# Causal attention with a routed feed-forward layer on one core: the masked key tiles of a head group move from its end to its start

## The reference, cut to what matters

```python
x = x + attention(layernorm(x), w_qkv, w_out)
x = x + ffn(layernorm(x), ...)

# attention: rotary position on q and k, then
scores = einsum('bhqd,bhkd->bhqk', q, k) * dh ** -0.5
scores = where(causal, scores, finfo.min)
out = einsum('bhqk,bhkd->bhqd', softmax(scores), v) @ w_out
# ffn: base_W product + a shared rank-16 pair + the best 2 of 6 routed rank-16 pairs, weighted by a softmax gate
```

## Time and profile before

| | |
|---|---|
| median of 3 runs | 338.3 us (334.99 to 338.99) |
| the profiled execution | 338.65 us |
| its span, first to last instruction | 336.9 us |
| exponentials (L465) | 272, one every 0.9 us where nothing holds them up |
| idle time of ACT before them | 40.1 us |

### The profile page before, as it was taken

How to read it: one execution, slowest core, us unless ns; L and a number is a source line. 1 busy time by engine, 2 the same in 40 slices (tenths; PEclk the granted TensorE clock), 3 DMA queues, 4 the chain that set the end, 5 groups by cost and what they waited for, 6 DMA issues and landing times.

```text
span 336.9 us, 6044 instructions
## 1 busy us (share of the span) xinstructions
PE 305.3 (91%) x2327; PEld 95.2 (28%) x2329; DVE 139.9 (42%) x406; ACT 270.1 (80%) x285; POOL 56.8 (17%) x134
## 2 busy tenths in 40 slices
PE   7968779897998999789999999999999999999985
PEld 2422222223333422223322312223122212421453
DVE  6863771597337557852651102002400400210463
ACT  9907375895978798698999999999999999899000
POOL 0524343030311300300303012003003003002000
PEclk9985997797999999999999999999999999999999
DMA  7260333022600010330000100000000000100001
GB/s 200 82 177 5 93 90 103 1 53 63 167 2 2 0 35 2 94 93 2 0 2 2 32 2 3 0 2 0 2 0 3 1 2 0 33 0 2 2 0 31
DMA packets 13586, 11.66 MB, mean 35 GB/s; under 512 B 1825, under 2 KB 12306, under 8 KB 13554
## 3 DMA queue, kind: packets, MB, share of 16 engines
q1 hardware_dynamic: 13410, 10.84, 11.7%
q0 software_dynamic: 144, 0.39, 0.4%
HBM read 3.88 MB, written 1.05 MB: 15 GB/s over the span
## 4 chain that ended last, share of the span: by engine, by line
PE 44%; DVE 22%; ACT 18%; issue 13%; DMA 2%; POOL 0%; DVEq 0%; ACTq 0%
PE po L745 18%; ACT pbuf L465 18%; PE ps L719 11%; DVE rest L526 3%; PE pm L782 3%; PE pm L768 2%; PE pm L771 2%; DVE rest L540 2%; PE ps L850 1%; DVE rot L532 1%; DVE xn L505 1%; PE pm L786 1%; PE pm L774 1%; DVE rot L519 1%; DVE parts L538 1%
## 5 line engine op out<-in xcount | busy, mean ns | idle before, releaser
L465 ACT ACTIVATE pbuf<-ps 128x1024 f32<-128x1024 f32 x272 | 253.9, 1122 | 40.1 <-PE ps L719 39.8
L745 PE MATMUL po<-pbuf,va 128*9 128x512 f32 (+3 forms) x1280 | 146.2, 541 | 1.7 <-DVE oT L513 1.3
L719 PE MATMUL ps<-qst,kst 64*128 64x512 bf16 (+3 forms) x640 | 99.2, 361 | 7.2 <-ACT pbuf L465 2.3
L444 POOL TENSOR_SCALAR_AFFINE_SELECT pbuf<-pbuf 128x256 f32<-128x256 f32 (+1 forms) x112 | 49.9, 461 | 242.1 <-ACT pbuf L465 241.5
L719 PEld LDWEIGHTS ps<-qst,kst 64*128 64x128 bf16 x640 | 25.3, 94 | 128.7 <-ACT pbuf L465 107.1
L513 DVE COPY oT<-po 128x512 f32<-128x512 f32 x16 | 11.0, 690 | 63.8 <-PE po L745 63.6
L745 PEld LDWEIGHTS po<-pbuf,va 128*9 128x9 f32 x1280 | 21.3, 89 | 49.9 <-issue 42.1
L587 DVE COPY xnT<-pm 128x512 f32<-128x512 f32 x12 | 8.3, 692 | 28.0 <-PE pm L768 28.0
L607 DVE RECIPROCAL rec<-pm 128x16 f32<-128x16 f32 x16 | 4.1, 258 | 34.7 <-PE pm L782 34.7
L850 PE MATMUL ps<-kst 128*128 128x512 bf16 x55 | 13.0, 379 | 0.2 <-issue 0.2
L771 PE MATMUL pm<-xnT,wqkv 128*128 128x512 f32 x16 | 10.1, 714 | 2.7 <-DVEq L636 2.7
(11 more groups left out here) (90 smaller groups left out, 181.6 us busy)
## 6 DMA issues: line engine op xcount, KB each, us to landing
kst<-parts SPq DMA_DIRECT2D x23, 128.0 KB, 2.5
qst<-parts SPq DMA_DIRECT2D x22, 128.0 KB, 2.4
xs<-x_dram SPq DMA_DIRECT2D x4, 256.0 KB, 3.4
cosT<-rope_c_dram SPq DMA_DIRECT2D x4, 256.0 KB, 4.2
sinT<-rope_s_dram SPq DMA_DIRECT2D x4, 256.0 KB, 4.8
out_dram<-xs SPq DMA_DIRECT2D x4, 256.0 KB, 2.3
wqkv<-w_qkv_dram SPq DMA_DIRECT2D x1, 320.0 KB, 4.1
qst<-parts POOLq DMA_DIRECT2D x2, 128.0 KB, 3.0
```

The costliest lines, as they stand in the source:

```text
L444: ins = nc.gpsimd.affine_select(out=edge, in_=edge, compare_op=ALU.is_ge, fill=0.0, base=0, pattern=[[0, edge.shape[1]], [1, P]], channel_ ...
L465: nc.scalar.activation(pbuf[:, u % NPB, :], ps[:, u % NS, :, :].rearrange("p b q -> p (b q)"), ACT.Exp, scale=SCALE).then_inc(exp_ready, 1)
L719: ins = nc.tensor.matmul(ps[:, u % NS, e, at * 2 * P + place:at * 2 * P + place + n], side(kst, e)[:, g * 2 + pair, key:key + P], side(qst ...
L745: ins = nc.tensor.matmul(po[32 * j:32 * j + DH + 1, q0:q0 + n], va[:, blk["kt"] + dk, head, :], pbuf[:, buf % NPB, at:at + n], start=blk[" ...
```

## The change

One line of the plan changes: within a group the order was old key tiles 0 to 4c-1, diagonal `full`, `ends`, `mid`. It is now diagonal `full`, `ends`, `mid`, then the old key tiles from 0 up. In chunk 0 there are no old tiles, and nothing changes. The number of units and blocks, `LAG`, the places of the jobs and of the evacuations, and every instruction's shape stay.

```diff
-            work = [("full", kt) for kt in range(4 * c + 1)] + [("ends", 4 * c + 1), ("mid", 4 * c + 2)]
+            work = [("full", 4 * c), ("ends", 4 * c + 1), ("mid", 4 * c + 2)] + [("full", kt) for kt in range(4 * c)]
```

## The result

The changed kernel took 343.24 us (median of 4 runs, 340.08 to 344.39), the kernel before beside it 338.36 us. The ratio is 1.0172, with a 95% interval of 1.0116 to 1.0228: slower, by 1.2 to 2.3%. The ratios leave out executions in a slower state and the medians do not, so a ratio is not the quotient of two medians (here 1.0144). The profiled execution took 343.01 us, its span is 341.3 us against 336.9.

What follows compares the result with a forecast made beforehand. ACT's exponentials (246 us) and 40 us of PE being late with scores were taken to bound the kernel; 1.0 + 0.6 + 1.9 - 0.3 + 0.2 = +3.4 us gave 341.7 us, eight-in-ten range 337.0 to 345.0.

Steps and rivals of the forecast that it cites:

- N10: Chunk 1: the wait before this job loses the block that filled it; PE idle 0.5 us, scores of 51 0.5 later.
- O0: Chunk 1: nothing stands in the wait for DVE's copy ahead of this job any more, so it runs 0.7 us later.
- K3: Chunk 2: a `full` ahead makes this job 0.4 us later; the term is +0.6, together with chunk 1 +1.6.
- ACT's wait at the gate: Chunk 2: ACT idles over 1 us ahead of the gate's exponential, where it had no idle time before.
- Rival B: Whole kernel: the waits take the change up, no effect, 338.3 us (336.5 to 339.8); chance 0.20.
- Rival C: Whole kernel: faster, with fewer mask waits and meetings and perhaps no half clock, 336 us (333 to 337.5); chance 0.10.
- Rival D: Whole kernel: slower by over 2%, clock falls in lengthened waits cost 1.4 us each, 346.7 us; chance 0.13.
- Chunk 1: Up to chunk 2's first exponentials: moved value products delay jobs; unit 72 comes 0.7 us later, the next ones 1.0.
- U0 and F0: End of chunk 1's jobs: 0.4 us comes back, because no `full` stands between them any more.
- N01 to R1: Chunk 2, units 99 to 114: bare waits and blocks ahead of jobs cost +1.9 us, together +3.5.
- Masks: Mask instructions meet DVE's work at other places: +0.2 us taken, with bounds of -0.4 and +1.0.
- The end: Last value products: the last is now a `full` that needs only the last exponential, no mask: -0.3 us.

Runs made afterwards that it cites:

- mid_early: Kernel before with `mid` moved behind old tiles 0 and 1 in chunks 1 to 3, other masks kept at the group's end, value products at odd units: ratio 1.0084.
- chunk1_only: Kernel before with the new order in chunk 1 alone: ratio 1.0022 (0.9991 to 1.0054).
- last_group_only: Kernel before with the new order only in the last group of the last chunk: ratio 0.9983 (0.9939 to 1.0027).
- mid_last: Kernel before with `full` and `ends` moved to the group's start, `mid` left last, full-width value products still at even units: ratio 1.0040.

## Why the prediction was right

**Direction and mechanism** held: slower, by 1.7% (the interval reaches beyond 2%), by the places of the value products. The bare waits at N10 (0.41 us) and O0 (0.52), the filled place ahead of K3, R0 1.15 later and ACT's wait at the gate (0.94, over 1 was forecast) are in the trace, and mid_early makes most of the loss with all masks but one in their old place. R1 came 4.7 us later, where 3.5 was forecast; the terms below say why. Rival B, the waits take it up, failed: chunk1_only keeps its 1.6 us to the end. Rival C failed as well, though two of its parts were true: the end, and KP2, whose instructions ran free of masks (0.69 for 1.00 us, 0.43 for 0.51). Against KP2 stands a meeting that the prediction had not listed, in chunk 2's first layer norm at 60 us: the three L316 there took 1.29 us for 0.49. Rival D's mechanism occurred once more than before, at V3. PE's wait there was longer (2.44 us for 2.15), but the fall can't be put down to that: without masks the new order waits 2.44 us too and keeps its clock, and in last_group_only it falls at a wait of 2.15. The block behind V3 took 0.84 us more (1.89 for 1.05), the stage 0.8 in last_group_only, for the 1.4 that D had priced. The step to "D would be the normal outcome" does not follow from the page that the prediction names: the waits in the example of the Trainium skill, "TensorE: Matmul & The Clock Gate", section "HAM oscillation — how this bites in real kernels", are 3 to 5 us long, longer than the waits at V2 and V3.

**Sizes.** The sum was +3.4 us; the profiled execution shows +4.4, the medians +4.9, the levels +4.7 (0.5). By its terms:

- Chunk 1, forecast +1.0: counted from unit 40, unit 73 is 1.6 later in the changed kernel and 1.5 without masks. The term was mis-sized by a third. Up to O0 it was right (98.81 to 99.28, and 0.2 from unit 40: the 0.7 forecast). Masks at M0 added 0.2, and at U0 and F0 the 0.4 did not come back whole: unit 72 is 1.2 later counted so, and not 0.7.
- K3, forecast +0.6 and 1.6 together: V3 is 1.63 later (141.71 for 140.08), which was luck in part. The stretch from unit 73 to 93 is 0.4 longer and not 0.6, which made up for the error in chunk 1. T3 is 1.46 later, the block ahead of K3 adds 0.38, and DVE's chain from K3 to V3 is 0.21 shorter, since its meeting with a mask is gone (a cast of 0.64 us is 0.43).
- Units 93 to 100, forecast 0: +0.5 in the changed kernel, with half clock behind V3, and 0.0 without masks and without that fall. mid_last, with full clock there, has +0.4. So the clock, the masks or both make it; this stays open.
- N01 to R1, forecast +1.9: between units 100 and 124 it is +2.35, and 1.90 between the two kernels without masks. The places were sized right. The rest is masks beside M1 (0.6 between units 114 and 121, with 0.2 less ahead of it).
- Masks, forecast +0.2 with bounds of -0.4 and +1.0: between -0.1 (0.7) by the levels and 1.0 by the stages. The forecast is not refuted as a sum, but its parts were wrong: I priced one instruction from the earlier trace rows and let the gain in KP2 stand against it. The layer norms have chains of short dependent instructions and four wider ones, and each one beside the masks of a new group had three or more of them lengthened (chunk 2's first, M0 and M1).
- Chunk 3, forecast 0: +0.1. The end, forecast -0.3: -0.43 in the last group, -0.3 net.

**The rule on the shared port.** The Trainium skill, "SBUF — State Buffer", section "SBUF: two separate sides", names VectorE instructions in a two-port mode, or with two SBUF inputs beside a GpSimd instruction that reads SBUF, as a mask does. The trace agrees on the second (L316: 0.40 for 0.16 us, with a mask from 104.11 to 104.52). L505, with one tensor input from SBUF, was 1.47 us for four instead of 1.11, and the two of the four that ran beside a mask were the long ones (0.55 and 0.49 for 0.34); whether it ran in such a mode no run here tells.

## What to carry to other kernels

In streams that are ordered by hand, work that fills the wait between two dependent jobs is worth what it fills. A reordering that keeps every instruction and every count can still empty such waits; look at each dependent pair in the engine's stream, before and after, for what stands between them. When a job is moved, look at what stands behind it on the other engine as well: one layer norm ahead of an evacuation cost all that a better place for V had won; with the norm behind it the kernel was 1.2% faster (0.6 to 1.8%). Stage by stage comparison of the profiled executions, from one marker instruction to another, resolved 0.1 us where timed runs spread over 8; but look first for a fall of the clock in the stages compared. Half of what first looked like the masks' share lies in a stage where one of the two executions had half clock.

## What was not expected of the hardware

Executions of one kernel spread over up to 8 us, and a large part of that goes with the granted clock: 0.27 us for each microsecond at half clock. The falls come at some of the long waits of PE (ahead of V2 1.95 us, ahead of V3 2.44 us, at an evacuation 3.32 us), in one execution at one and in the next at another. Leaving out the masks of chunks 1 to 3 on GpSimd, whose own time is nearly hidden, made the kernel 2.4 us (0.3) faster. About half of it is found, in VectorE's longer instructions and in the wait of the last products.
